# Last chunk's weighting moved to VectorE, four weight loads moved ahead, and filler products, in a fused attention and expert layer

## The reference

```python
x = x + attn(spikes(x, cond), ...)      # delta rule, three FIR paths, then "mix"
# mix: five paths per head, gate from their statistics
logits = gelu(gate_in @ gW1 + gb1) @ gW2 + gb2            # per token, 4 heads x 5 paths
probs = softmax(logits / tau) * (1 - sum(eps)) + eps
o = einsum('blhp,blhpd->blhd', probs, paths)
o = o * rsqrt(mean(o * o) + 1e-5) * norm_w ; x = x + o @ Wo
# gated recurrence over the 1024 steps, z = x
gate = sigmoid(h @ Wh.T + z_t @ Wz.T + b) ; h = tanh(h * (1 - alpha) + gate * z_t)
# experts: top-1 of 8 by hs @ gate_w.T, each relu(h @ w1[e].T + b1[e]) @ w2[e].T + b2[e]
x = x + experts(hs)
```

## Time and profile before

| | |
|---|---|
| median of 3 runs | 976.74 us (975.64 to 977.39) |
| profiled execution, its time | 978.99 us |
| its span, first to last instruction | 977.2 us |
| mean granted TensorE clock | 0.864 |
| busy over the span | PE 73%, DVE 70%, ACT 54%, POOL 30% |
| Mix ends, the recurrence starts | 600.96 us |
| experts start | 762.74 us |
| first hidden product of the experts | 792.10 us |

### The profile page before, as it was taken

How to read it: one execution, slowest core, us unless ns; L and a number is a source line. 1 busy time by engine, 2 the same in 40 slices (tenths; PEclk the granted TensorE clock), 3 DMA queues, 4 the chain that set the end, 5 groups by cost and what they waited for, 6 DMA issues and landing times. The chain is left out here.

```text
span 977.2 us, 16350 instructions
## 1 busy us (share of the span) xinstructions
PE 714.4 (73%) x6072; PEld 412.9 (42%) x6072; DVE 684.8 (70%) x954; ACT 530.9 (54%) x978; POOL 293.1 (30%) x242
## 2 busy tenths in 40 slices
PE   2840008786756367783876888999999859999995
PEld 1310004333546366773443444444445624455542
DVE  5999985967744989257589771999999425444442
ACT  5888764753422343655553435999997214443332
POOL 0000000001102000000042440898988055565661
PEclk9985558988898758898879879999998579999998
DMA  5640000001892000000200013900000731111100
GB/s 201 219 138 0 0 0 22 1 0 25 230 250 55 3 2 2 25 3 16 86 0 1 22 43 108 399 19 1 0 0 1 253 121 40 40 42 40 45 25 7
DMA packets 35457, 60.78 MB, mean 62 GB/s; under 512 B 7755, under 2 KB 22091, under 8 KB 34994
## 3 DMA queue, kind: packets, MB, share of 16 engines
q1 hardware_dynamic: 30194, 51.32, 16.5%
q0 software_dynamic: 2880, 6.30, 2.1%
q10 hardware_dynamic: 2304, 2.10, 0.6%
HBM read 54.46 MB, written 6.82 MB: 63 GB/s over the span
## 5 line engine op out<-in xcount | busy, mean ns | idle before, releaser
L1995 ACT ACTIVATE xT<-x_tr,moe_b 128x64 f32<-128x64 f32 x320 | 67.7, 361 | 116.0 <-PE x_tr L1960 115.9
L1160 POOL TENSOR_TENSOR path<-path,mix_pr 128x1280 f32<-128x1280 f32 x16 | 38.7, 2446 | 147.0 <-DVE mix_pr L1394 147.0
L1934 PE MATMUL x_hid<-w,moe_xt 128*64 x160 | 74.8, 611 | 1.0 <-DVE moe_xt L2093 0.8
L1937 PE MATMUL x_hid<-h,moe_xt 128*64 128x512 f32 x160 | 74.8, 611 | 0.0
L1948 PE MATMUL x_y<-w,xT 128*64 x320 | 73.3, 382 | 1.8 <-ACT xT L1995 1.8
L1951 PE MATMUL x_y<-hs,xT 128*64 128x256 f32 x320 | 73.3, 382 | 0.0
L1714 DVE TENSOR_TENSOR_SCAN w<-r_bank,w 128x512 f32<-128x512 f32 x56 | 69.7, 1246 | 0.2 <-ACT r_bank L1648 0.2
L218 PE MATMUL bad_sum<-spike_bad,ones 128*128 128x16 f32 x2 | 0.6, 385 | 84.3 <-ACT spike_outside L184 84.3
L1588 PE MATMUL r_bank<-recur_h_other,w1h 128*128 128x512 f32 x128 | 60.3, 593 | 0.7 <-ACT recur_h_other L1628 0.7
L1584 PE MATMUL r_bank<-hs,eye 128*128 128x512 f32 x112 | 57.2, 592 | 1.8 <-DVE h L1695 1.8
L214 PE MATMUL w_bank<-spike_wbuf,spike_pick 128*128 128x512 f32 x80 | 39.5, 649 | 22.9 <-DMA spike_wbuf<-in_gW 22.9
(11 more groups left out here) (292 smaller groups left out, 1984.7 us busy)
## 6 DMA issues: line engine op xcount, KB each, us to landing
spike_wbuf<-in_gW SPq DMA_DIRECT2D x8, 1280.0 KB, 6.2
w<-in_w1T SPq DMA_DIRECT2D x8, 1024.0 KB, 12.1
w<-in_w2T SPq DMA_DIRECT2D x8, 1024.0 KB, 14.8
fir_band<-in_band_l SPq DMA_DIRECT2D x11, 512.0 KB
fir_band<-in_band_m SPq DMA_DIRECT2D x11, 312.0 KB
mix_st<-in_band_l SPq DMA_DIRECT2D x5, 512.0 KB
xT<-in_xT SPq DMA_DIRECT2D x4, 512.0 KB, 6.5
xT<-in_xT SPq DMA_DIRECT2D x2, 1024.0 KB, 6.3
```

The lines of the kernel that those rows point to most:

```text
L1160: nc.gpsimd.tensor_tensor(x, x, w, ALU.mult).then_inc(s.weighted, 1)
L1934: nc.tensor.matmul(hid_bank[n][side(0), :], xt[:, c, side(0)], m.w1[:, bass.ds(e, 1), c, cols].rearrange("p o n -> p (o n)"), start=(c == ...
L1937: last = nc.tensor.matmul(hid_bank[n][side(1), :], xt[:, c, side(1)], w1_copy[:, g % 2, c, cols], start=(c == 0), stop=(c == C - 1), skip_ ...
L1995: nc.scalar.activation(ht[:, k, side(x)], turned[:, side(x)], ACT.Relu, bias=b1[:, bass.ds(e[x], 1), k]).then_inc(s.ht_ready, 1)
```

## The change

- In Mix, VectorE multiplies the last chunk's four tiles itself (`weigh`), in turn with its other work; GpSimd does the first twelve only.
- Wz has a tile of its own (`wz`), loaded at Mix's start; `m.wg` keeps Wh. The gate parts and row turns stand elsewhere in the lists of TensorE and ScalarE. ScalarE does one Sigmoid on a single column behind the last root.
- In the recurrence, four guesses are made first and the other four one by one behind the first four Sigmoids. TensorE's first product doesn't wait for the leak constants.
- SP issues second weights of experts 2 and 3 once all residuals and slopes are done, of 6 and 7 once the last states are moved; the experts' block loads 4 and 5.
- `keep_clock` does products of the identity and a tile of ones into a bank that nobody reads: 5 behind the verdict's product, 1 behind each of 12 turns, 20 behind the slot products.
- Three of the last turns come before the slot products, two stay between. The row stores are issued by SP, behind its loads, not by ScalarE.

```diff
+def keep_clock(nc, m, bank, times):
+    for _ in range(times):
+        nc.tensor.matmul(bank[:, 0:P], m.eye[:], m.ones[:], start=True, stop=True)
...
+            sp.dma_start(wz[:], d.wgT[D:].rearrange("(k p) n -> p k n", p=P)).then_inc(s.wg_in, 16)
             sp.wait_ge(s.hid_psum, 4 * CHUNKS)
-            sp.dma_start(m.wg, d.wgT.rearrange("(k p) n -> p k n", p=P)).then_inc(s.wg_in, 16)
+            sp.dma_start(m.wg, d.wgT[0:D].rearrange("(k p) n -> p k n", p=P)).then_inc(s.wh_in, 16)
...
-            for a in range(CHUNKS * TILES):
+            for a in range(LAST * TILES):
...
-            turned_back(2)
             zw_out(0)
+            turned_back(2)
             rows_out(0)
             root(3)
             zw_out(1)
+            turned_back(3)
             rows_out(1)
             root(4)
-            turned_back(3)
+            nc.scalar.activation(warm[:], m.bias_g[:, 0:1], ACT.Sigmoid)
+            turned_back(4)
+            rows_out(2)
             zw_out(2)
-            rows_out(2)
-            turned_back(4)
             rows_out(3)
             zw_out(3)
...
-            project(2)
             gate_part(0)
+            project(2)
             rows(0)
             gate_part(1)
+            project(3)
             rows(1)
-            project(3)
-            gate_part(2)
+            project(4)
             rows(2)
-            project(4)
+            gate_part(2)
             rows(3)
             gate_part(3)
...
+            def weigh(a):
+                nc.vector.tensor_tensor(by_head(a), by_head(a), weights(a), ALU.mult).then_inc(s.last_weighted, 1)
...
+            dve.wait_ge(s.probs_ready, CHUNKS)
+            weigh(12)
+            weigh(13)
             combine(12)
             combine(13)
             residual(2)
             squares(3)
+            weigh(14)
+            normed(3)
+            weigh(15)
             combine(14)
             combine(15)
-            normed(3)
             squares(4)
             normed(4)
...
+            def load_w2(e0):
+                for e in (e0, e0 + 1):
+                    sp.dma_start(m.w2[:, e], d.w2T[e].rearrange("(k p) n -> p k n", p=P)).then_inc(m.w2_in, 16)
+            sp.wait_ge(s.res_ready, ALL)
+            sp.wait_ge(s.sq_ready, ALL)
+            load_w2(W2_AHEAD)
+            sp.wait_ge(s.h_ready, UNITS + ALL)
+            load_w2(W2_AHEAD + 4)
...
-            pe.wait_ge(s.leaks, 5)
...
+                if u == 0:
+                    pe.wait_ge(s.leaks, 5)
...
+            keep_clock(nc, m, bank[2], 5)
             pe.wait_ge(s.verdict, 3)
...
             for u in range(ALL + LAG_F):
                 if u < ALL:
                     sigmoid(u)
+                if u + GUESSED < UNITS:
+                    guess(u + GUESSED)
...
-        TURNED, TURNED_LAST = 2, 5
+        TURNED, TURNED_LAST = 2, 2
...
-            for e in range(W2_AHEAD, E):
-                sp.dma_start(w2[:, e], d.w2T[e].rearrange("(k p) n -> p k n", p=P)).then_inc(s.w2_in, 16)
+            for e in (W2_AHEAD + 2, W2_AHEAD + 3):
+                sp.dma_start(w2[:, e], d.w2T[e].rearrange("(k p) n -> p k n", p=P)).then_inc(m.w2_in, 16)
+            for a in range(TILES):
+                sp.wait_ge(s.row_ready, a + 1)
+                sp.dma_start(m.h_rows[a * P:(a + 1) * P, :], row[:, a, :]).then_inc(s.rows_out, 16)
...
             for a in range(TURNED, TILES - TURNED_LAST):
                 turn(a)
+                keep_clock(nc, m, spare_bank, 1)
...
-                if a % 3 == 2:
-                    turn(TILES - TURNED_LAST + a // 3)
+                if a in (1, 3):
+                    turn(TILES - TURNED_LAST + a // 2)
             last.then_inc(s.slot_psum, 1)
+            keep_clock(nc, m, spare_bank, 20)
...
-                act.wait_ge(s.row_ready, a + 1)
-                act.dma_start(m.h_rows[a * P:(a + 1) * P, :], row[:, a, :]).then_inc(s.rows_out, 16)
```

More of the change, by code:

```diff
@@ L1100, in mix @@
         wo = sb("wo", [P, C, D])
+        wz = sb("wz", [P, C, D])
         nw = sb("nw", [P, 1])
@@ L1124, in mix @@
         path = lambda a: m.path[:, a]
+        by_head = lambda a: path(a).rearrange("q p (h v) -> q p h v", v=DV)
+        weights = lambda a: (pr[a // TILES % 2][:, a % TILES].rearrange("q h p -> q p h").unsqueeze(3)
+                             .broadcast_to([P, NP, H, DV]))
         where = lambda n: (n // (T // N), (n % (T // N)) * N)
@@ L1154, in _ @@
         def _(pool):
-            for a in range(CHUNKS * TILES):
[L1156 to L1160, removed]
+            for a in range(LAST * TILES):
+                pool.wait_ge(s.probs_ready, a // TILES + 1)
+                nc.gpsimd.tensor_tensor(by_head(a), by_head(a), weights(a), ALU.mult).then_inc(s.weighted, 1)
         @block.scalar
@@ L1314, in gate_part @@
                     for k in range(C):
-                        last = nc.tensor.matmul(hid_bank[c][:], m.wg[:, C + k, c * P:(c + 1) * P],
+                        last = nc.tensor.matmul(hid_bank[c][:], wz[:, k, c * P:(c + 1) * P],
                                                 m.xT[:, k * B + b, t0:t0 + N], start=(k == 0), stop=(k == C - 1))
@@ L1340, in _ @@
                 logits(i)
+            gate_part(0)
             project(2)
-            gate_part(0)
             rows(0)
             gate_part(1)
+            project(3)
             rows(1)
-            project(3)
+            project(4)
+            rows(2)
             gate_part(2)
-            rows(2)
-            project(4)
             rows(3)
@@ L1398, in combine @@
                 x = path(a)
-                dve.wait_ge(s.weighted, a + 1)
+                if n < LAST:
+                    dve.wait_ge(s.weighted, a + 1)
+                else:
+                    dve.wait_ge(s.last_weighted, k + 1)
                 nc.vector.tensor_tensor(x[:, 0:2], x[:, 0:2], x[:, 2:4], ALU.add).then_inc(s.adding, 1)
@@ L1624, in _, with guess @@
         def _(act):
-            for u in range(UNITS):
+            def guess(u):
                 b, t0, c = unit(u)
@@ L1629, in _ @@
                                      scale=0.5).then_inc(s.h_ready, 1)
+            for u in range(GUESSED):
+                guess(u)
             act.wait_ge(s.leaks, 2)
@@ L1816, in experts @@
         y_bank = own.enter_context(nc.psum_tensor("x_y", [P, D], F32))
-        names = ("zeros", "w2_in", "rows_out", "cleared", "r", "count_psum", "slots_ready", "slot_psum",
+        spare_bank = own.enter_context(nc.psum_tensor("x_spare", [P, N], F32))
+        names = ("zeros", "rows_out", "cleared", "r", "count_psum", "slots_ready", "slot_psum",
                  "tokens_ready", "eid_ready", "turned", "row_ready", "picked", "x_psum", "xt_ready", "hid_psum", "hid_ready",
```

14 lines of the change are left out of this document (9 added, 5 removed).

## The result

The changed kernel takes **967.43 us** (median of 4 runs, 965.46 to 969.41), against 976.19 for the kernel before: a ratio of 0.9884, 95% interval 0.9858 to 0.991. The profiled execution took 969.41 us with a span of 967.6, at a mean granted clock of 0.873. The forecast was 962.5, range 957 to 972: the sign and the range were right, but of the 14.2 us forecast only 8.8 came.

A forecast was written before the change was run, and what follows sets the result against it. Bounds: GpSimd's multiplications and contention at Mix's end, full TensorE and VectorE in the sweeps, then the low clock and saturated DMA. −3.9 + 0.9 + 0.3 − 11.5 = −14.2 us gives 962.5, range 957 to 972.

The forecast's parts named there:

- Mix, −3.9: Mix's end: VectorE multiplying the last four tiles itself ends the last gate part at 595.7 instead of 599.8; −3.9 us.
- Sweeps' start, +0.9: Recurrence's start: GpSimd's wait for all eight guesses delays unit 3's argument despite the saved table loads; +0.9 us.
- only VectorE's own pace counts, so the loss stays: In the sweeps, TensorE's possible 1.4 us of catching up was said not to help, leaving +0.9 us.
- Block end, +0.3: Behind the sweeps: five fillers behind the verdict's product let TensorE's drain end later; +0.3 us (0 to 1.5).
- Experts' head, −11.5: Experts' start to block 1: fewer loads, earlier rows, slots and fetch, full clock start block 1 at 787.8; −11.5 us.
- The reason given for the clock's rise: Experts' turns: TensorE's clock rises near 769 because this is the first stretch there without a gap in TensorE.
- the signs named for a wrong forecast: A hidden product still waiting for DMA of second weights or rows, fillers at 0.43 us each, table loads in the sweeps.
- Stores behind loads: Experts' start: rows wait behind weight loads moving at 239 GB/s, landing at 786.3; head only −1.2, 972.8 us; chance 0.09.
- Fillers outlast the fetch: Experts' start: clock falls in slot products, about half of twenty fillers cost 0.43 us; head −6.5, 967.5 us; chance 0.16.
- The clock stays low: Clock low until the hidden products: head +2.0, Mix +1.3, total +4.5, 981.2 us; chance 0.11 including a late rise.
- Multiplications at 2.5: Mix: VectorE's multiplications take 2.5 us each, so Mix gains 0; 966.5 us; chance 0.07.
- clock held through Mix: Mix: TensorE's clock doesn't fall before the last projection, so Mix gains 7 us; 959.4 us; chance 0.09.

The follow-up runs named there:

- Experiment 8: Changed kernel with Mix as before (GpSimd's multiplications, old order, no early Sigmoid), the rest of the change kept; 975.07 us in one run.
- experiment 11: The changed kernel run again without any edit, beside two later variants on one chip; 963.81 us, ratio 0.9875 to the kernel before.
- experiment 4: Changed kernel with all eight guesses ahead of the first sigmoid; 963.9 us, ratio 0.9872 to the kernel before.
- experiment 2: Changed kernel with all six second-weight loads at the experts' start, ahead of the row stores on SP's queue; 975.77 us, ratio 0.9996 to the kernel before.
- experiment 12: Changed kernel with all guesses first, VectorE's first second-weight copy behind block 0's turned tokens, and no fillers; 966.27 us, ratio 0.9907 to the kernel before.
- experiment 9: Changed kernel with all guesses first, row stores before the last two loads, these behind the first tokens, weight copies later; 963.0 us, ratio 0.9866 to the kernel before.
- Experiment 6: Changed kernel with VectorE's first copy of second weights behind its copy of block 0's turned tokens; 968.73 us in one run.
- Experiment 7: Changed kernel with 36 fillers behind the slot products instead of 20; 965.52 us in one run.
- experiment 1: Changed kernel without any of its 37 filler products; 965.0 us, ratio 0.9899 to the kernel before.
- 10: The three small edits on the changed kernel: all guesses first, VectorE's first second-weight copy behind block 0's turned tokens, 28 fillers instead of 20; 961.98 us, ratio 0.9843.
- experiment 3: Changed kernel with the row stores issued by ScalarE again, the loads still ahead; 967.5 us, ratio 0.9911 to the kernel before.

## Why the prediction was right, and where not

**Mix, −3.9: right in size, by luck: two errors cancel.** (The forecast's own sum gives 599.8 − 595.7 = 4.1, not 3.9.) Multiplications at 1.48 (I took 1.4) and no contention on VectorE. ScalarE's first square stood behind the rows' copies by more than I had allowed (VectorE rests 1.38 us for it): 1.2 of the 1.5 us by which the last part was late. TensorE rested 3.27 us before the last projection as forecast, but the low clock caught only the projection: from the turns to the last gate part's end it took 13.3 us (584.30 to 597.56) where I had 14.7 (581.0 to 595.7). Experiment 8 gives the part 3.5 by itself, and the change run again (experiment 11) has 3.3.

**Sweeps' start, +0.9: 0.0.** The steps came as forecast: no table loads, first product 1.29 us behind the start (forecast 1.25), GpSimd's residual at 12.92 (12.86). Unit 3's argument came at 15.26 (forecast 15.1). What failed is "only VectorE's own pace counts, so the loss stays". The pace was not fixed: from unit 3's argument to unit 55's it was 2.537 us a unit instead of 2.551, which gives back 0.7 us, and from there to the check VectorE took 4.86 instead of 5.20. Which engine allows the faster pace no run shows; VectorE's own argument took 0.67 us where it had taken 0.67 to 0.70. The early start was not worthless: experiment 4 shows that an earlier GpSimd does shorten the recurrence, by 1.27. So the part is a gain of 1.3 from the tables and a loss of 1.3 from the split guesses.

**Block end, +0.3: +0.1 in the table, +0.2 by the fillers.** (3.01 us from the verdict's product to the first turn before, 3.20 after, 3.03 without fillers.)

**Experts' head, −11.5: −7.5. This is the step that failed.** The four loads ahead do what was forecast: no product waits for weights, and without them (experiment 2) the whole gain is gone. TensorE's list went as forecast too: the last row is copied 11.7 us behind the first turn (forecast 11.6) and the slot products run at the full clock. The reason given for the clock's rise, no gap in TensorE, is not shown by that: the router's products before ran 7.00 us without one and stayed low, and so did the turns of experiment 12. Behind that every term but the fillers' was too small:
- The last row's store: "copied at 774.4, stored by 777.3" is 2.9 us; it took 4.2 (772.3 to 776.5). The loads are through near 769 (forecast 770), by the count of bytes and by the rate, which then rises from 350 to 380 GB/s; but the rows that were issued meanwhile wait behind them in the same queue, and the last one waits for that backlog. Without loads in front it takes 3.1 (experiment 9).
- From the last store's landing to the fetch: I had 0.3, it is 1.0.
- The tokens: I took 3.15 us from the earlier trace rows; they take 4.23, because VectorE's copy, which waits for loads and rows, now starts in the same moment as GpSimd's fetch, which waits for the rows. Before, it was held until the last load at 789.55, two microseconds behind the fetch. Experiment 6 takes this away: 1.0 us.
- Fillers: I had them 0.5 us late; they ended 2.7 us before the tokens. Behind them TensorE rested 2.7 us, the clock fell, and block 0 took 7.0 us as before, not the 5.4 "at full clock". Experiment 7 holds the clock and has 5.35.

Together they are 1.3 + 0.7 + 1.1 − 0.6 + 1.6 = 4.1 (the −0.6 is the fillers' 0.5 and 0.1 between turn and first product), the 29.08 us measured less the 25.0 of the forecast (787.8 − 762.8). One of the signs named for a wrong forecast half came: the way to the first product still leads through the store of the last row, though not through second weights, and the fetch is 7.9 us earlier against the first turn, not near 10. The cast, held 1.0 us by GpSimd's copy, cost nothing in the end, since the rows landed 0.4 us behind it.

**The rivals.** *Stores behind loads* is real, and the loads did not move at 387 GB/s but at 350; yet with two loads in front it costs 1.0 us here (the last store takes 4.06 us, and 3.10 in experiment 9), not 10, and with six in front (experiment 2) the fetch waits 12.4 us. *Fillers outlast the fetch*: not here; in experiment 8 they did, and it cost nothing since block 0 gained as much. *The clock stays low*: with the fillers it rose in every trace (and fell back in the slot products of experiment 8), without them in one of two (and there too it fell back in the slot products). Experiment 12 is that case, and against it the fillers are worth 4.1 us; against experiment 1, 0.5. What decides whether it rises without them I can't say. *Multiplications at 2.5* did not come (1.48), *clock held through Mix* only in part.

**Left open.** Why the stages ahead end between 559.5 and 566.0 from trace to trace, and whether the three small edits beat the change in whole time, where 1.8 us were measured and the intervals overlap. The block-0 clock is also not settled: it was low for a part of block 0 in nine traces and full in five (4, 7, 8, 9, 10), in 4 without any edit of that stage.

## What to carry to other kernels

When two waits that end together are removed, work out what the freed work will now start at the same moment: here VectorE's copy of the weights, held by the loads before, met GpSimd's fetch once the loads were early, and cost it 1 us. A store behind loads pays for what is queued before it, and from its landing to GpSimd's fetch another 1.0 us passed (TensorE's turn started 0.14 us behind the tokens' landing). Filler products are priced against the case in which the clock doesn't rise without them: one run in which it does makes them look worthless.

## What the runs showed of the hardware

- While loads moved alone, the rate was 350 GB/s at a DMA share of 1.1; from 770 to 774, where by the count of bytes only row stores were left, it was 379. The 387 of the earlier trace rows was read where both ran, and is no measure for loads alone.
- SyncE was busy 11.54 us with six issues of 1 MB in a row and 0.99 with two; of the four loads ahead the first two took it 1.00, the other two, issued 2.4 us later, 2.22.
- A cast of 128x20 took 0.18 us alone and 1.12 to 1.36 beside GpSimd's copy of 128x2048 (0.39 where that copy ended sooner, in experiment 3); the issue of an indirect DMA 1.23 alone and 2.24 beside VectorE's copy of the same shape.
- Right behind a rest TensorE still ran at the full clock, and fell later: behind 3.27 us in Mix the turns took 0.66 and then the projection 3.47 (1.99 at full); behind 2.67 us in the experts the turn took 0.41, the first hidden product 0.82, the next three 1.06 (0.59 at full).
